# Feed-forward part three steps later, weight preparation spread over eight steps

## The reference

```
xx = x shifted by one token - x;  xr, xv, xg, xk = x + xx * mix
r, v, k = xr @ W_r.T, xv @ W_v.T, xk @ W_k.T;  g = sigmoid(xg @ W_g.T)
state = state * w + k v^T;  attn_t = state @ r_t          (a scan over the 1024 tokens)
y = layernorm((attn * g) @ W_o.T) * gamma + beta
x1 = layernorm(x + y)
q(t): blocks of 16: scale = max|t| / 6, values rounded to 0, .5, 1, 1.5, 2, 3, 4, 6, times scale
gate, up = q(x1) @ q(w_gate).T, q(x1) @ q(w_up).T          (704 hidden features)
out = layernorm(x1 + q(silu(gate) * up) @ q(w_down).T)
```

## Time and profile before

| | us |
|---|---|
| median of three runs | 659.39 (658.94 to 662.06) |
| the profiled execution | 656.57 |
| its span, first to last instruction | 654.6 |
| mean granted TensorE clock | 0.959 of full |

### The profile page before, as it was taken

The page is one execution under the profiler, slowest core; times in us unless marked ns, Lnnn a source line. Parts: engine busy times, 40 slices in busy tenths (PEclk is TensorE's granted clock), DMA queues, the critical chain, the costliest instruction groups (busy, mean ns, idle before and its releaser), DMA issues.

```text
span 654.6 us, 14594 instructions
## 1 busy us (share of the span) xinstructions
PE 569.1 (87%) x5120; PEld 477.9 (73%) x5120; DVE 510.9 (78%) x1506; ACT 277.2 (42%) x637; POOL 330.4 (50%) x471
## 2 busy tenths in 40 slices
PE   1468589999999999999999999999999999987754
PEld 1356467888878888888888888888888888876643
DVE  2988667888878888888888888888788888778751
ACT  1235255444444455444445444444445544432211
POOL 2234344555555555555555555555565555544321
PEclk9687689999999999999999999999999999999896
DMA  7300000000000000000000000000000000000000
GB/s 191 102 2 1 9 10 3 1 18 17 19 17 18 18 17 19 18 17 18 17 11 9 17 18 19 18 17 17 18 18 18 9 11 10 9 10 10 9 9 20
DMA packets 14046, 13.13 MB, mean 20 GB/s; under 512 B 2576, under 2 KB 13712, under 8 KB 13968
## 3 DMA queue, kind: packets, MB, share of 16 engines
q1 hardware_dynamic: 13968, 12.13, 6.2%
HBM read 7.93 MB, written 4.19 MB: 19 GB/s over the span
## 4 chain that ended last, share of the span: by engine, by line
PE 79%; DVE 9%; ACT 5%; POOL 2%; issue 2%; DMA 1%; SPq 0%; DVEq 0%; POOLq 0%; ACTq 0%
PE bank L734 20%; PE bank L867 14%; PE bank L677 9%; PE bank L752 9%; PE bank L716 4%; PE bank L804 4%; PE bank L759 4%; PE bank L769 4%; PE bank L859 3%; ACT hq_t L591 3%; PE bank L704 2%; DVE mix L1044 2%; PE bank L694 1%; POOL rstd L353 1%; PE bank L814 1%
## 5 line engine op out<-in xcount | busy, mean ns | idle before, releaser
L371 POOL TENSOR_SCALAR_AFFINE_SELECT scores<-scores 128x512 f32<-128x512 f32 x128 | 89.0, 708 | 81.0 <-ACT scores L508 80.4
L867 PE MATMUL bank<-down_t,hq_t 128*128 128x256 f32 x384 | 94.1, 396 | 21.6 <-ACT hq_t L591 21.6
L353 POOL TENSOR_TENSOR rstd<-veps,neg_half 128x1 f32<-128x1 f32 x96 | 77.8, 810 | 66.9 <-DVE veps L994 66.1
L867 PEld LDWEIGHTS bank<-down_t,hq_t 128*128 128x128 f32 x384 | 72.0, 194 | 38.3 <-ACT hq_t L591 29.4
L1044 DVE SCALAR_TENSOR_TENSOR mix<-shift,mu,x_t 128x128 f32<-128x128 f32 x256 | 82.5, 374 | 2.6 <-POOL shift L380 2.6
L508 ACT COPY scores<-bank 128x512 f32<-128x512 f32 x128 | 68.8, 590 | 34.5 <-PE bank L677 32.7
L752 PE MATMUL bank<-mix,proj_t 128*128 128x128 f32 x512 | 70.2, 295 | 10.5 <-DVE mix L1044 10.5
L734 PE MATMUL bank<-gu_hi,xq_hi 128*128 128x352 f32 x256 | 68.4, 349 | 11.2 <-DVE late L1092 6.4
L380 POOL TENSOR_TENSOR shift<-x_t 128x256 f32<-128x256 f32 x32 | 20.1, 629 | 112.6 <-ACT x_t L529 111.3
L752 PEld LDWEIGHTS bank<-mix,proj_t 128*128 128x128 f32 x512 | 66.1, 209 | 12.1 <-DVE mix L1044 11.1
L677 PE MATMUL bank<-r_par,rv 32*128 32x256 f32 x512 | 72.5, 400 | 0.8 <-ACT scores L508 0.8
(11 more groups left out here) (123 smaller groups left out, 1160.2 us busy)
## 6 DMA issues: line engine op xcount, KB each, us to landing
x_tok<-in_L_attn_x_dram SPq DMA_DIRECT2D x32, 128.0 KB, 2.3
out_dram<-late_down SPq DMA_DIRECT2D x32, 128.0 KB, 1.7
late_down<-in_L_ffn_w_down_dram SPq DMA_DIRECT2D x1, 704.0 KB, 8.6
late<-in_L_ffn_w_gate_dram SPq DMA_DIRECT2D x1, 640.0 KB, 7.1
late<-in_L_ffn_w_up_dram SPq DMA_DIRECT2D x1, 640.0 KB, 7.3
scores<-in_L_attn_W_r_dram SPq DMA_DIRECT2D x1, 256.0 KB, 5.0
scores<-in_L_attn_W_v_dram SPq DMA_DIRECT2D x1, 256.0 KB, 5.3
scores<-in_L_attn_W_g_dram SPq DMA_DIRECT2D x1, 256.0 KB, 5.5
```

The costliest lines, as they stand in the source:

```text
L353: g.tensor_tensor(rstd[:, i:i + 1], veps[:, i:i + 1], neg_half, ALU.pow).then_inc((rstd_ready, x_rstd, y_rstd)[i], 1)
L371: g.affine_select(out=a, in_=a, compare_op=ALU.is_ge, fill=0.0, base=0, pattern=[[0, 4], [1, P]], channel_multiplier=-1).then_inc(s_masked, 1)
L867: mm = t_.matmul(B_PA[:, 0:C], hq_t[:, t.c % 2, j], down_t[:, j], start=(j == 0), stop=(j == NH - 1))
```

## The change

Between the quantisation of x1 (lag 4) and its use, three steps are put in: everything that stood at lag 5, 6 and 7 stands at lag 8, 9 and 10, on all engines and in SyncE's stores, so there are 42 steps for 39. x1 and xq get eight slots each. The waits that name FFN tiles are shifted to match.

Weight preparation: pieces 0 and 1 are quantised after step 0; pieces 2 to 7 one per step in steps 1 to 6, each of the seven operations in the place of the same operation of `hgrid`, which has no tile yet. GpSimd dequantises them inside its step, behind `shift`. TensorE's turns stand after step 3 (gate), 6 (up) and 7 (down). ScalarE moves each gate or up bank twice, to `gu_hi` and in full to the new `gu_full`, and VectorE makes `gu_lo` from these two after step 4 (gate) and step 7 (up).

The first tile's x is transposed and copied before the tables; the table transposes go to another bank; VectorE's wait for `tabs_moved` moves behind step 0. The general form keeps lag 5 and does all of the preparation after step 0.

```diff
+FFN = 3
-LAG_MAX = 7
+LAG_MAX = 7 + FFN
+def turn_at(stage, general):
+    return 0 if general else (3, 6, 7)[stage]
...
+        gu_full = sb("gu_full", [P, KC, HID])
-        x1 = sb("x1", [P, 4, C])
+        x1 = sb("x1", [P, TPB, C])
-        xq = sb("xq", [P, 2, C])
+        xq = sb("xq", [P, TPB, C])
... GpSimd, step
+                    if not general and t.b == 0 and t.c:
+                        for n in (0, 1) if t.c == 1 else (t.c,):
+                            dequantize(n)
+                        if t.c == len(pieces) - 1:
+                            pad_hidden()
-                t = tile(7)
+                t = tile(7 + ffn)
                 if t is not None:
                     rstd_of(t, 2, general)
... ScalarE
+            move_x(Tile(0, 0))
             act.wait_ge(ipow_tr, 1)
-            s.copy(ipow, B_T[:, 0:C]).then_inc(tabs_moved, 1)
+            s.copy(ipow, B_O[:, 0:C]).then_inc(tabs_moved, 1)
... move_gate_up
+                wait(act, gu_lo_ready, KC * m)
                 for k in range(KC):
                     for lo, hi in ((0, 512), (512, HID)):
                         act.wait_ge(w_tr, n + 1)
-                        s.copy(gu_hi[:, k, m * HID + lo:m * HID + hi], w_bank[n % 2][:, 0:hi - lo]
-                               ).then_inc(gu_hi_ready, 1)
-                        act.wait_ge(w_moved, n + 1)
+                        cols = slice(m * HID + lo, m * HID + hi)
+                        s.copy(gu_hi[:, k, cols], w_bank[n % 2][:, 0:hi - lo]).then_inc(gu_hi_ready, 1)
+                        s.copy(gu_full[:, k, lo:hi], w_bank[n % 2][:, 0:hi - lo]
+                               ).then_inc(w_moved, 1)
                         n += 1
... TensorE
             pe.wait_ge(const_step, 6)
+            transpose_x(Tile(0, 0), False)
             pe.wait_ge(exceeds_ready, 1)
...
-            def early(c):
-                if c in (2, 3):
-                    turn_gate_up(c - 2)
-                if c == 4:
-                    pe.wait_ge(ln_step, 4)
-                    turn_down()
-                    pe.wait_ge(w_moved, 13 + NH)
+            def early(c, general):
+                for stage, turn in enumerate((lambda: turn_gate_up(0), lambda: turn_gate_up(1),
+                                              turn_down)):
+                    if c == turn_at(stage, general):
+                        if c >= 4:
+                            pe.wait_ge(ln_step, LN * (c - 4) + 4)
+                        turn()
+                        pe.wait_ge(w_moved, (9, 13, 13 + NH)[stage])
+                        if stage == 2:
+                            pe.wait_ge(gu_lo_ready, 4)
... TensorE, step (the same for tile(6), and on ScalarE, VectorE and SyncE)
-                t = tile(5)
-                if t is not None:
-                    gate_up(t, 0)
+                t = tile(5 + ffn)
+                if t is not None:
+                    gate_up(t, 0, ffn)
... VectorE
             def low_parts(m):
-                for n in range(4 * m, 4 * m + 4):
-                    k, part = n % 4 // 2, n % 2
-                    lo, hi = m * HID + 512 * part, m * HID + (HID if part else 512)
-                    dve.wait_ge(gu_hi_ready, n + 1)
-                    v.tensor_tensor(gu_lo[:, k, lo:hi], w_bank[(n + 1) % 2][:, 0:hi - lo],
-                                    gu_hi[:, k, lo:hi].bitcast(F32), ALU.subtract
-                                    ).then_inc(w_moved, 1)
+                dve.wait_ge(w_moved, 9 + 4 * m)
+                for k in range(KC):
+                    cols = slice(m * HID, (m + 1) * HID)
+                    v.tensor_tensor(gu_lo[:, k, cols], gu_full[:, k],
+                                    gu_hi[:, k, cols].bitcast(F32), ALU.subtract
+                                    ).then_inc(gu_lo_ready, 1)
+            def early(c, general):
                 if c == 0:
-                    dve.wait_ge(ffn_loaded, 16 * 3)
-                    weights(2, 3)
-                if c == 1:
-                    weights(4, 5)
...
+                    dve.wait_ge(tabs_moved, 5)
+                    for n in range(0, len(pieces) if general else 2, 2):
+                        for k in range(QN):
+                            quantize(n, k)
+                            quantize(n + 1, k)
+                for m in range(2):
+                    if c == (0 if general else (4, 7)[m]):
+                        low_parts(m)
...
                 def hgrid(k):
+                    if not general and t0 is not None and t0.b == 0 and 0 < t0.c < len(pieces) - 1:
+                        quantize(t0.c + 1, k)
                     if t6 is None:
                         return
```

More of the change, by code:

```diff
@@ L47, in count, with first @@
         return min(value, per_tile * B * TPB) if isinstance(value, int) else value
+    def first(self):
+        return isinstance(self.b, int) and self.b == 0 and self.c == 0
     def affine(self, per_batch, more):
@@ L314, in step @@
                     sp.dma_start(x_tok[:, t.c, :], x_rows[t.count(1, 0)]).then_inc(x_in[t.c], 16)
-                t = tile(7)
+                t = tile(7 + FFN)
                 if t is not None:
@@ L453, in run @@
                     pool.wait_ge(pow_reset, 1)
-                run_tiles(pool, lambda tile: step(tile, general), general, early=early)
+                run_tiles(pool, lambda tile: step(tile, general), general,
+                          early=early if general else None)
             pool.wait_ge(flag_ready, 2)
@@ L520, in step @@
                 o_used, u_used = (attn_ready, attn_ready) if general else (o_done, u_done)
+                ffn, x_slots = (0, 4) if general else (FFN, TPB)
                 t = tile(0)
-                if t is not None:
[L523 to L529, removed]
-                t = tile(5)
+                if t is not None and not t.first():
+                    move_x(t)
+                t = tile(5 + ffn)
                 if t is not None:
@@ L597, in _ @@
             either_path(act, flag, lambda general: run_tiles(
-                act, lambda tile: step(tile, general), general, early=early))
+                act, lambda tile: step(tile, general), general,
+                early=lambda c: early(c, general)))
         @blk.tensor
@@ L603, in _, with transpose_x @@
             t_ = nc.tensor
+            def transpose_x(t, general):
+                wait(pe, x_in[t.c], t.affine(16, 16))
+                wait(pe, x_moved, t.count(1, 0))
+                wait(pe, v_tok_ready, t.count(1, -1))
+                wait(pe, xq_t_ready, t.count(1, -5 - (0 if general else FFN)))
+                for k in range(KC):
+                    mm = t_.transpose(B_T[:, k * P:(k + 1) * P],
+                                      x_tok[:, t.c, k * P:(k + 1) * P], ident)
+                mm.then_inc(x_tr, 1)
             pe.wait_ge(const_step, 6)
+            transpose_x(Tile(0, 0), False)
             pe.wait_ge(exceeds_ready, 1)
@@ L788, in step @@
                 t = tile(0)
[L789 to L797, removed]
+                if t is not None and not t.first():
+                    transpose_x(t, general)
                 t = tile(4)
@@ L872, in _ @@
             either_path(pe, flag, lambda general: run_tiles(
-                pe, lambda tile: step(tile, general), general, early=early))
+                pe, lambda tile: step(tile, general), general,
+                early=lambda c: early(c, general)))
         @blk.vector
@@ L946, in _ @@
                                 ).then_inc(tab_step, 1)
[L948 to L960, removed]
@@ L972, in early, with quantize @@
-            def early(c):
-                if c == 0:
-                    dve.wait_ge(ffn_loaded, 16 * 3)
-                    weights(2, 3)
-                if c == 1:
-                    weights(4, 5)
[L978 to L981, removed]
-                    low_parts(1)
+            def quantize(n, k):
+                w = pieces[n]
+                rows, cols = w.shape
+                if k == 0:
+                    wait(dve, q_ready, n - 3)
+                    if n in (0, 3):
+                        dve.wait_ge(*((gate_loaded, 16 * 2), (ffn_loaded, 16 * 3))[n // 3])
+                if k == 3:
+                    wait(dve, q_ready, n - 1)
+                grid(k, w, q_grid[0:rows, n % 2, 0:cols], cols // BLK, q_scale[:, n % 4],
+                     q_inv[:, n % 4], q_mag[:, n % 2], q_step[n % 2], lambda i: QN * (n // 2) + i)
@@ L1032, in step @@
             def step(tile, general):
-                t0, t1, t4, t5, t6, t7 = (tile(lag) for lag in (0, 1, 4, 5, 6, 7))
+                ffn = 0 if general else FFN
+                t0, t1, t4 = (tile(lag) for lag in (0, 1, 4))
+                t5, t6, t7 = (tile(lag + ffn) for lag in (5, 6, 7))
                 def mix_of(i):
@@ L1200, in run @@
                     v.memset(scan_sum, 0.0).then_inc(scan_step, 1)
-                dve.wait_ge(gate_loaded, 16 * 2)
-                weights(0, 1)
```

(3 more changed lines are left out.)

103 lines of the change are left out of this document (58 added, 45 removed).

## The result

The changed kernel takes 679.88 us (median of 4 runs, 675.47 to 681.07), the kernel before 659.70 beside it: ratio 1.0287, 95% interval 1.0235 to 1.034. Slower, by 20 us; forecast were 675 us and +16. The profiled execution took 681.07 with a span of 679.3.

A forecast was written before the change was run, and what follows sets the result against it. TensorE's own matmuls bound the middle steps (17.50 us), so only the two ends could move. First FFN step at 121.9 - 89.45 - 15.8 = +16.6, rounded down to +16: 672.6 us profiled, 675 us median, range 664 to 685.

The forecast's parts named there:

- The frame: Whole kernel: middle steps stay 17.50 us; faster only if the first FFN step starts before 105.3 us, against 89.45 before.
- The head: Eight attention-only steps with all weight preparation, up to the first FFN step: forecast to end at 121.9 us.
- Steps 1 to 3: Head: step 1 takes 5.6 us, to 33.1; steps 2 and 3 take 9.0 each, mixes of step 3 done at 51.
- rival D: Head: VectorE's mixes slowed beside GpSimd's dequantisation, 2.0 us more in six steps, +12 more, 687 us; chance 0.06.
- Step 7: Last attention-only step: 15.4 us with no piece and turns in TensorE's idle end, plus low parts of up 1.7: 17.1.
- rival C: Cold tail: clock falls in FFN-only steps, +1.6 to +4.2 us in each of three, +21 to +29, 684 us; chance 0.09.
- four FFN-only steps of 12.2: Tail: a sign that the forecast is right, each FFN-only step lasting 12.2 us as step 36 did before.
- -15.8: From the first FFN step on: three middle steps fewer (-52.5 us) and three FFN-only steps more (+36.7 us).
- + 3 x 12.23: Tail: three more FFN-only steps, each priced like step 36 of before, with TensorE's clock full: +36.7 us.
- Rival A: Head: turns and earlier scores keep TensorE's clock up in some of steps 4 to 7; +11, 670 us; chance 0.20.
- Rival B: Head: preparation fills waits in steps 1 to 7, VectorE's bare work of 101 us binds; -4, 655 us; chance 0.07.
- The rule weighed: Head: each new attention-only step starts cold and stays at 15.4 us; otherwise the four give up to 2.5 each.

The follow-up runs named there:

- tail_busy: The changed kernel with filler products on TensorE in the steps without scores and ahead of the last tile's transposes: 670.29 us.
- lag0_spread: The changed kernel with FFN back at lag 5 and pieces 2 to 7 quantised in pairs in steps 1 to 3: 657.49 us, ratio to before 0.997.
- x_first: The kernel before with only the first tile's x transposed early, step 0's mixes ahead of the first weight pair: 655.91 us, ratio 0.9949.
- lag0_two_full: Against lag0_spread, a second gu_full buffer and both low parts moved into step 4: 652.48 us, ratio to before 0.9905.
- lag3_no_quant: The changed kernel without VectorE's and GpSimd's weight quantisation operations, raw weights turned and used: 670.20 us, ratio to before 1.0184.
- lag3_two_full_busy: The changed kernel with a second gu_full buffer, low parts before the first norm of steps 4 and 7, and tail fillers: 667.28 us, ratio to before 1.0154.

## Why the prediction was right, point by point

The frame held. Middle steps last 17.5 as before; the kernel is slower because eight attention-only steps take more than 105.3 us.

The head: 121.9 forecast, 122.71 measured (120.02 in tail_busy, whose head is the same), but some of that is luck, errors that cancel. Step 0's mixes end at 19.59 (19.7), the first pair at 27.3 (27.5). Steps 1 to 3 took 27 us, not 23.5: in step 3 the mixes waited 1.49 for GpSimd's shift, which came at 45.98 only, when step 2's scores were through TensorE, ScalarE (x copied at 45.71) and GpSimd's masks, and mixes beside a dequantisation were slow (1.83 for two). That is some of rival D, on the path; but TensorE's own step 3 and its turn weren't behind VectorE, and L843 came at 56.58 (57.4). Step 4's rest 16.1 (16.6), with the low parts 2.11 and not 1.7. Steps 5 and 6 took 15.08 and 15.98 (15.4 each). Step 7 took 18.97 and not 17.1: the mis-sized term is "turns of step 6 and 7 lie in TensorE's idle end of a step". The up turn ran over: TensorE came to L843 1.8 us after attn started (105.54 against 103.74), and cold (1.92).

```profile
99.88 0.97 PE L680 MATMUL bank<-ident,late 128*128 128x128 f32 x6
...
102.79 0.97 PE L680 MATMUL bank<-ident,late 128*128 128x128 f32 x6 [1.94 <-ACT gu_full L521]
...
105.54 1.92 PE L843 MATMUL bank<-proj_t,attn 128*128 128x256 f32 x4
```

The tail is where the remaining error is, and it is one of mechanism: the sign that I had named for C, slow products in several tail steps, is there, and "four FFN-only steps of 12.2" isn't. I took the FFN-only steps at 12.23 and gave rival C 0.09. In the profiled execution C came true in part, +5.7 in the four steps, which is nearly all of the 7.2 us by which "-15.8" was off (556.6 us from the first FFN step on, for 565.2 before: -8.6); tail_busy settles that it was the clock. The argument against C, that step 36 of before had kept its clock at 1.00, was one step of one execution, and the exception: of the 21 FFN-only steps in the profiles of the kernels without fillers in the tail, before aside, 20 lasted 13.4 to 15.6 us and one 12.23 (step 39 of the changed kernel). Step 36 itself took 13.4 in lag0_spread and 15.6 in x_first and in lag0_two_full. So the term mis-sized is "+ 3 x 12.23": steps 36 to 39 took 54.7 for 48.9.

The medians hide part of that. The profiled execution came out 8.5 us above its forecast (681.07 for 672.6), the median 4.9 (679.88 for 675): to come from one to the other I had added the 2.8 by which before's profiled run lay below its median, and the changed kernel's lay 1.2 above. That is scatter, and it fell my way.

Rival A (warm head): in step 6 a warm start is worth 0.9 us, as A's 15.0 for that step says; for step 5 it wasn't tested, and for 7 and 8 it is open. Rival B (not slower): refuted by lag3_no_quant; a bound made of VectorE's work alone was not the head's bound.

The rule weighed, from the Trainium skill's page "TensorE: Matmul & The Clock Gate", Part 1, is that the half rate is the default state and activity releases it. The traces agree in both ends: L843 took 1.92 in step 7 after idling, L778 3.68 in step 38. It weighed more in the tail (8.4 us by tail_busy), where I hadn't applied it, than in the one step of the head that could be read, step 6 (0.9 us).

## What to carry to other kernels

To put a part of a pipeline some steps later adds a filling step at the front and a draining step at the back for each full step that it takes away: -17.5 against 15 to 19 and 12 to 16 here. It pays only if the filling steps hide work that stood bare, and what was hidden here had stood bare for less than that: putting the preparation back into blocks cost 8 us, the lag some 20. The preparation could be hidden without the lag, once a second buffer and earlier low parts took out the waits that the new layout had brought in. That kernel came out 0.9% below the kernel before, 1.6% with fillers in the tail, where the change came out 2.9% above.

And a step's price that is read from one step of one execution should be looked for in other executions first, above all where TensorE idles in it.

## What the runs showed of the hardware

A few filler products of TensorE in idle stretches of 1.5 to 2 us kept its clock at 2.4 GHz (1.00 granted in steps 36 to 39, for 0.87, 0.78, 0.87 and 1.00) and took 9.6 us off the changed kernel's median. The kernel before scattered from 654.62 to 662.08 over 24 runs; lag0_two_full from 648.99 to 655.12 over 10, with fillers from 645.29 to 648.67 over 4. By and large the shorter runs of each kernel are those with the higher mean granted clock (before: 654.62 at 0.962, 662.08 at 0.951). That fits a tail whose clock falls in some executions at other places than in others, but wasn't tested apart.

The same two instructions of VectorE on 704 columns from two buffers took 2.11 us at a step's end (changed kernel, 70.65) and 1.69 in front of the first norm (lag3_two_full_busy, 55.40). At the step's end GpSimd worked beside them: its xq (L441) started at 70.81 and took 1.20, where it took 0.62 at 87.73. In front of the norm it did nothing meanwhile. That the one slows the other is likely, not tested.
